# First norm of an image block: centring and variance moved between engines, and third-stage weights loaded in contiguous runs

## What is computed

```python
x = x + conv_ref(ln_c(x), ...)          # ln_c: norm over the 96 channels, eps 1e-6, no weights
t = to_tokens(x); x = from_tokens(t + ffn_ref(ln_t(t), W1, b1, W2, b2))
# conv_ref(v): crops of 16x16 pixels at a step of 14
#   y = layernorm(crop) * norm1_w + norm1_b            # eps 1e-5
#   4-head attention inside each crop, wproj, added back, overlaps averaged -> x2
#   y = gelu(layernorm(x2) @ fc1_w + fc1_b); dw = gelu(conv5x5(y) + dw_b)
#   result (y + dw) @ fc2_w + fc2_b + x2
# ffn_ref: values rounded to 8-bit (5 exponent bits) before each product, relu between W1 and W2
```

## Time and profile before

| | |
|---|---|
| runs | 9153.25, 9166.02, 9173.01 us; median 9166.02 |
| profiled execution | 9185.78 us, span 9184.0 us, mean granted TensorE clock 0.95 |
| busy share of the span | PE 87%, DVE 57%, ACT 51%, POOL 23% |
| first stage | 0 to 896 us |
| attention stage | 896 to 4599 us |
| third stage, head without strips | 4599 to 4709 us |
| third stage, strips | 4709 to 9184 us |

### The profile page before, as it was taken

One profiled execution on the slowest core, in us unless ns is written; L12 is line 12 of the kernel. 1 busy time (PEld: TensorE's weight loads), 2 busy tenths in 40 slices (PEclk: granted clock), 3 DMA queues, 4 the chain that ended last, 5 costly groups with the idle time before them and its releaser, 6 DMA issues.

```text
span 9184.0 us, 208496 instructions
## 1 busy us (share of the span) xinstructions
PE 8035.3 (87%) x76932; PEld 4839.5 (53%) x76932; DVE 5221.1 (57%) x9929; ACT 4672.3 (51%) x8702; POOL 2150.5 (23%) x1712
## 2 busy tenths in 40 slices
PE   6776899999999999999858989989989888998998
PEld 3333444444444444444445566666666666666665
DVE  5565677777777777777633444444444444444444
ACT  2221555555555555555525555555555555555554
POOL 0000333333333333333301211212111121121111
PEclk8888899999999999999969999999999999999999
DMA  4333343333433334333251111111111111111110
GB/s 119 113 114 104 88 98 87 91 94 84 100 83 94 94 84 98 86 92 94 71 45 34 44 40 34 44 40 35 43 40 43 35 43 41 34 44 40 35 43 24
DMA packets 480819, 612.84 MB, mean 67 GB/s; under 512 B 173263, under 2 KB 415697, under 8 KB 455317
## 3 DMA queue, kind: packets, MB, share of 16 engines
q1 hardware_dynamic: 480260, 605.46, 26.8%
HBM read 395.81 MB, written 166.64 MB: 61 GB/s over the span
## 4 chain that ended last, share of the span: by engine, by line
PE 28%; DVE 9%; ACT 7%; issue 5%; SPq 1%; DVEq 0%; ACTq 0%; DMA 0%; POOLq 0%; POOL 0%
PE P L1285 6%; PE P L1151 5%; PE P L1298 5%; PE P L1206 4%; ACT H L1358 4%; DVE H L1522 3%; PE P L1159 3%; DVE H L1515 2%; PE P L1314 2%; DVE Z L1537 2%; PE P L1125 1%; ACT Z L1383 1%; ACT L1383 1%; ACT L1346 1%; SPq L991 1%
## 5 line engine op out<-in xcount | busy, mean ns | idle before, releaser
L812 DVE TENSOR_REDUCE NM<-P 128x2 f32<-128x512 f32 x2888 | 1858.6, 686 | 719.2 <-PE P L645 714.3
L759 ACT ACTIVATE PROB<-P 128x512 f32<-128x512 f32 x2888 | 1491.1, 603 | 1090.7 <-PE P L660 1090.7
L1206 PE MATMUL P<-FC,XN 97*126 97x192 f32 x5408 | 1101.1, 343 | 15.7 <-ACT Y L1368 14.8
L1206 PEld LDWEIGHTS P<-FC,XN 97*126 97x126 f32 x5408 | 944.3, 197 | 167.9 <-issue 77.9
L660 PE MATMUL P<-QF,KS 32*128 32x256 f32 x11552 | 869.5, 417 | 94.0 <-DVE QF L806 93.2
L660 PEld LDWEIGHTS P<-QF,KS 32*128 32x128 f32 x11552 | 544.5, 192 | 642.0 <-DVE QF L806 506.6
L496 POOL TENSOR_TENSOR Y<-XHS,RNS 96x512 f32<-96x512 f32 x304 | 600.7, 2007 | 931.9 <-DMA RNS<-rnorm 931.9
L1352 ACT ACTIVATE SQ<-Z 96x512 f32<-96x512 f32 x260 | 163.8, 630 | 1286.5 <-DVE Z L1502 1286.5
L668 PE MATMUL P<-PROB,V 128*32 128x256 f32 x11552 | 797.8, 395 | 2.4 <-ACT PROB L759 1.5
L1368 ACT ACTIVATE Y<-P 126x384 f32<-126x384 f32 x1352 | 705.9, 570 | 109.2 <-PE P L1206 103.6
L1092 POOL TENSOR_TENSOR T<-T,Y 96x512 f16 (+1 forms) x260 | 299.2, 1151 | 1722.7 <-DVE Y L1526 1722.7
(11 more groups left out here) (141 smaller groups left out, 12209.9 us busy)
## 6 DMA issues: line engine op xcount, KB each, us to landing
RBC<-sums SPq DMA_DIRECT2D x456, 160.0 KB, 3.1
X<-x2map SPq DMA_DIRECT2D x52, 1344.0 KB, 8.4
XHS<-xhat SPq DMA_DIRECT2D x76, 768.0 KB, 6.4
RNS<-rnorm SPq DMA_DIRECT2D x38, 1536.0 KB, 9.2
x2map<-XHS SPq DMA_DIRECT2D x76, 768.0 KB
T<-in_x SPq DMA_DIRECT2D x52, 960.0 KB
out<-T SPq DMA_DIRECT2D x52, 960.0 KB, 4.9
X<-in_x SPq DMA_DIRECT2D x32, 1536.0 KB, 13.3
```

What stands on the lines that cost most here:

```text
L759: A.activation(PROB[:, par, u, :], P[:, B_ST[u], :], ACT.Exp, scale=DQ ** -0.5).then_inc(act_exp, 1)
L812: V_.tensor_reduce(NM[:, :, 32 * u + DQ], P[:, B_S[u], :].rearrange("p (a m) -> p a m", a=2), axis=AX.X, op=ALU.max).then_inc(dve_max, 1)
L1206: m = M.matmul(P[0:KW, 5 + (r + 2) % 3, i * MLP:(i + 1) * MLP], xnf[:, RI * WX * w:RI * WX * w + KW], FC1[:, :], start=True, stop=True)
```

## The change

**First stage.** TensorE multiplies the chunk by `CENW`, the identity minus 1/96 (made once by VectorE), and so has x minus mean in PSUM at once. ScalarE copies it out of PSUM to XH and squares it from PSUM to SQ; VectorE's `centre` is gone. The variance products go out four at a time, to 32 PSUM rows each (column groups), one bank; ScalarE copies the bank to SBUF (`VS`), and one product with `REP` sums the four groups and gives the three copies. Block i's spread products stand between the centring and variance products of block i+1 in TensorE's order. VectorE multiplies into buffers of their own (`XO`), and its second reciprocal comes behind the multiplications; ScalarE's second root of block i stands in the middle of block i+1. SP loads X for block i+3 once block i+1 has been centred (block i+2 before), and stores xhat before rnorm.

**Third stage.** W1, W2 and the filter are loaded as they lie (20 loads instead of 22), turned by eight fp32 transposes on TensorE into PSUM, and cast from there by VectorE; the tap products wait for those casts. The constants `stat` and `bcast` are gone; the first stage uses `pick`, `rep` and `spread` of the third.

```diff
+            def fetch(par, i):
+                b, j = where(i)
+                sp.dma_start(X[par][:, :], xv[:, b, bass.ds(j * TOK, TOK)].rearrange("c a n -> c (a n)")).then_inc(x_loaded[par], 16)
+
+            def keep(par, i):
+                b, j = where(i)
+                hold(sp, sp_passed, dve_xh, i * 8 + 8)
+                sp.dma_start(xhat[:, b, bass.ds(j * TOK, TOK)].rearrange("c a n -> c (a n)"), XO[par][:, :]).then_inc(stored[par], 16)
+                hold(sp, sp_passed, dve_rn, i + 1)
+                sp.dma_start(rv[:, b, bass.ds(j, 1), :].rearrange("c a i n -> c (a i n)"), RCP[0:NCH, 1, :]).then_inc(r_stored, 16)
+
+            sp.wait_ge(pe_cen, 8)
+            fetch(0, 2)
+            with sp.Fori(0, nblk // 2 - 2) as k:
                 for par in range(2):
                     i = k * 2 + par
+                    hold(sp, sp_passed, pe_cen, i * 8 + 16)
+                    fetch(1 - par, i + 3)
+                    keep(par, i)
...
+            def spread(i, j):
+                if j == 0:
+                    pe.wait_ge(dve_parts, i + 1)
+                if j >= 2:
+                    pe.wait_ge(dve_xh, i * 8 + (j - 1))
+                for c in (2 * j, 2 * j + 1):
+                    m = T.matmul(P[0:C, B_BC + j % 2, (c % 2) * CW:(c % 2 + 1) * CW], BSEL[:, c, :], RB[:, :], start=True, stop=True)
+                m.then_inc(pe_bc, 1)
+            def body(par, i, k):
+                pe.wait_ge(x_loaded[par], k * 16 + 16)
+
+                def centred(j):
+                    T.matmul(P[0:C, j % 4, :], CENW[:, :], X[par][:, pair(j)], start=True, stop=True).then_inc(pe_cen, 1)
+
+                def variance(q):
+                    pe.wait_ge(act_sq, i * 8 + (2 * q + 2))
+                    for g in range(4):
+                        c = 4 * q + g
+                        m = T.matmul(P[32 * g:32 * g + 32, B_VAR, 0:CW], SSEL[:, NV - 1 - c:NV - 1 - c + 32],
+                                     SQ[:, c // 2 % 4, (c % 2) * CW:(c % 2 + 1) * CW], start=(q == 0), stop=(q == 3))
+                    m.then_inc(pe_var, 1)
 
                 for j in range(4):
-                    mean(j)
-                for j in range(8):
-                    pe.wait_ge(act_sq, i * 8 + (j + 1))
-                    for c in (2 * j, 2 * j + 1):
-                        m = T.matmul(P[0:C, 4 + par, 0:CW], SSEL[:, c, :], SQ[:, j % 4, (c % 2) * CW:(c % 2 + 1) * CW],
-                                     start=(c == 0), stop=(c == NCH - 1))
-                    m.then_inc(pe_var, 1)
-                    if j < 4:
-                        pe.wait_ge(dve_cen, i * 8 + (j + 1))
-                        mean(j + 4)
-
...
+            def second_std(i):
+                act.wait_ge(dve_step, i * VSTEPS + 3)
+                if not first(i, 1):
+                    act.wait_ge(dve_rn, i)
+                A.activation(STD[:, 1, :], VR[:, :], ACT.Sqrt, bias=EPS[:, 1:2]).then_inc(act_std2, 1)
+
+            def body(par, i, k):
+                if not first(i, 2):
+                    act.wait_ge(dve_xh, i * 8 - 8)
                 for j in range(8):
-                    act.wait_ge(dve_cen, i * 8 + (j + 1))
+                    act.wait_ge(pe_cen, i * 8 + (j + 1))
+                    A.activation(XH[par][:, pair(j)], P[0:C, j % 4, :], ACT.Copy)
                     if j >= 4:
-                        act.wait_ge(pe_var, i * 8 + (j - 3))
-                    A.activation(SQ[:, j % 4, :], XH[par][:, pair(j)], ACT.Square).then_inc(act_sq, 1)
-                act.wait_ge(pe_var, i * 8 + 8)
-                A.activation(STD[:, :], P[0:C, 4 + par, 0:CW], ACT.Sqrt, bias=EPS[:, 0:1]).then_inc(act_std, 1)
-                act.wait_ge(dve_step, i * VSTEPS + 3)
-                A.activation(STD[:, :], VR[:, :], ACT.Sqrt, bias=EPS[:, 1:2]).then_inc(act_std, 1)
-
-            pipeline(act, front, lambda par, i: None)
+                        act.wait_ge(pe_var, i * 4 + (j // 2 - 1))
+                    A.activation(SQ[:, j % 4, :], P[0:C, j % 4, :], ACT.Square).then_inc(act_sq, 1)
+                    if j == 3 and not first(i, 1):
+                        second_std(i - 1)
+                act.wait_ge(pe_var, i * 4 + 4)
+                A.activation(VS[:, :], P[:, B_VAR, 0:CW], ACT.Copy).then_inc(act_vs, 1)
+                act.wait_ge(pe_rep, i + 1)
+                A.activation(STD[:, 0, :], P[0:C, B_STAT, 0:CW], ACT.Sqrt, bias=EPS[:, 0:1]).then_inc(act_std, 1)
+
+            blocks(act, body)
+            second_std(nblk - 1)
...
+            V.tensor_tensor(CENW[:, :], CENW[:, :], MEANW[:, :], ALU.subtract)
             V.tensor_copy(BSEL[:, :, :], BSEL32[:, :, :]).then_inc(dve_init, 1)
 
-            def centre(par, i):
-                for j in range(8):
-                    dve.wait_ge(pe_mean, i * 8 + (j + 1))
-                    V.tensor_tensor(XH[par][:, pair(j)], X[par][:, pair(j)], P[0:C, j % 4, :], ALU.subtract).then_inc(dve_cen, 1)
...
-                dve.wait_ge(act_std, i * 2 + 2)
-                if not isinstance(i, int) or i > 0:
-                    dve.wait_ge(r_stored, i * 16)
-                V.reciprocal(RCP[:, 1, :], STD[:, :]).then_inc(dve_rn, 1)
-
-            def back(par, i):
+                if not first(i, 2):
+                    dve.wait_ge(stored[par], k * 16)
                 for j in range(8):
                     dve.wait_ge(pe_bc, i * 8 + (j + 1))
-                    V.tensor_tensor(XH[par][:, pair(j)], XH[par][:, pair(j)], P[0:C, 6 + j % 2, :], ALU.mult).then_inc(dve_xh, 1)
-
-            centre(0, 0)
-            chain(0, 0)
-            with dve.Fori(0, nblk // 2 - 1) as k:
-                i = dve.snap(k * 2)
-                dve.wait_ge(stored[1], k * 16 + 16)
-                centre(1, i + 1)
-                back(0, i)
-                chain(1, i + 1)
-                dve.wait_ge(stored[0], k * 16 + 16)
-                centre(0, i + 2)
-                back(1, i + 1)
-                chain(0, i + 2)
-            dve.wait_ge(stored[1], (nblk // 2) * 16)
-            centre(1, nblk - 1)
-            back(0, nblk - 2)
-            chain(1, nblk - 1)
-            back(1, nblk - 1)
+                    V.tensor_tensor(XO[par][:, pair(j)], XH[par][:, pair(j)], P[0:C, B_BC + j % 2, :], ALU.mult).then_inc(dve_xh, 1)
+                dve.wait_ge(act_std2, i + 1)
+                if not first(i, 1):
+                    dve.wait_ge(r_stored, i * 16)
+                V.reciprocal(RCP[:, 1, :], STD[:, 1, :]).then_inc(dve_rn, 1)
+
+            blocks(dve, body)
...
-            with nc.allow_non_contiguous_dma(reason="weights, once"):
-                load(DW[0:25, :], dww.rearrange("c a y x -> (a y x) c"))
-                load(W1R, w1.rearrange("n k -> k n"))
-                for f in range(3):
-                    load(W2R[:, f, :], w2[:, f * 128:(f + 1) * 128].rearrange("n k -> k n"))
+            load(DWN, dww.rearrange("(h c) a y x -> c h (a y x)", h=2))
+            load(W1N, w1.rearrange("(f n) k -> n f k", f=3))
+            load(W2N, w2)
...
+            for f in range(3):
+                M.transpose(P[0:C, f, 0:128], W1N[:, f, :], IDN[:, :])
+                M.transpose(P[:, 3 + f, 0:C], W2N[:, f * 128:(f + 1) * 128], IDN[0:C, 0:C])
+            for h in range(2):
+                t = M.transpose(P[0:25, 6, h * C:(h + 1) * C], DWN[:, h, :], IDN[0:C, 0:C])
+            t.then_inc(pe_turn, 1)
+            pe.wait_ge(dve_step, 1)
...
-            V.tensor_copy(W1Q[:, :], W1R, saturate=False)
-            V.tensor_copy(W2Q[:, :, :], W2R, saturate=False)
+            dve.wait_ge(pe_turn, 1)
+            V.tensor_copy(W1Q[:, :].rearrange("k (f n) -> k f n", f=3), P[0:C, 0:3, 0:128], saturate=False)
+            V.tensor_copy(W2Q[:, :, :], P[:, 3:6, 0:C], saturate=False)
+            V.tensor_copy(DW[0:25, :], P[0:25, 6, 0:MLP])
```

More of the change, by code:

```diff
@@ L44, in norm_stage @@
         XH = [sb(f"XH{i}", [C, TOK]) for i in range(2)]
+        XO = [sb(f"XO{i}", [C, TOK]) for i in range(2)]
         SQ = sb("SQ", [C, 4, 2 * CW])
-        STD = sb("STD", [C, CW])
+        VS = sb("VSA", [128, CW])
+        STD = sb("STD", [C, 2, CW])
         VR = sb("VR", [C, CW])
@@ L110, in _ @@
+                    fetch(1 - par, i + 3)
+                    keep(par, i)
+            for i in range(nblk - 4, nblk):
+                if i + 3 < nblk:
+                    sp.wait_ge(pe_cen, i * 8 + 16)
+                    fetch((i + 3) % 2, i + 3)
+                keep(i % 2, i)
             sp.wait_ge(r_stored, 16 * nblk)
             for par in range(2):
-                sp.wait_ge(stored[par], 16 * (nblk // 2 + par))
-        def pipeline(eng, front, back):
-            front(0, 0, None)
+                sp.wait_ge(stored[par], 16 * (nblk // 2))
@@ L117, in pipeline, with blocks @@
+        def blocks(eng, body):
+            body(0, 0, 0)
+            body(1, 1, 0)
             with eng.Fori(0, nblk // 2 - 1) as k:
                 i = eng.snap(k * 2)
-                front(1, i + 1, k)
-                back(0, i)
```

(46 more changed lines are left out.)

68 lines of the change are left out of this document (28 added, 40 removed).

## The result

The changed kernel takes **9362.34 us** (median of 4 runs, 9278.71 to 9380.12) beside 9159.64 us for the kernel before on the same chip: ratio 1.0195, 95% interval 1.0152 to 1.0238. It is slower by about 2% (1.5 to 2.4), where 8704 us and a clear gain were forecast. Its profiled execution took 9361.24 us, span 9359.4, mean granted clock 0.902 (0.95 before).

The account below looks back on a forecast made before the run. The first stage was taken as bound by a dependence loop through three engines, the third stage's head by weight loads. Savings of 416 and 46 us, 462 together, gave 8704 us from the median 9166.02; 80% range 8665 to 8800.

Parts of the forecast that it names:

- First stage: Term for the first stage: it ends at 479.6 us in place of 895.9, 416 us less.
- a walk of 13.91: First stage, step-by-step estimate of one block's dependence loop through the engines: 13.91 us a block.
- DMA pace: Rival, first stage: loads and stores set the pace, 15 us a block, +34 us, 8738; blocks stretched to 16 had 0.19.
- column groups in a row: Rival, first stage: variance column groups don't overlap, 1.72 us a group, 16.9 a block, +93 us, 8797; chance 0.06.
- clock in this stage: Rival, first stage: TensorE stays at 1.2 GHz for all (+220, 8924) or a third (+70, 8775) of each block; chance 0.09.
- table loads: Rival, first stage: ScalarE's Copy and Square evict each other, 16 loads a block, 127 us slower than before, 9293.
- Head of the third stage: Term for the third stage's start: weights land 49.5 us sooner, 3 us lost again, 46 us less; bounds 40 and 52.
- Attention 3703 as before: Attention stage: its code is kept, so it stays 3703 us long.
- The step that failed: Attention and the rest of the third stage, strips included: they keep their code, so no time was added for them.
- The two foreseen terms: First stage 416 us less and third stage's weights 46 us less, together 462 us.
- table loads or another loss: Case for the whole kernel: slower than before through ScalarE's table loads in the first stage or another loss; chance 0.02.

Follow-up runs that it names:

- run 10: The kernel before with 214 empty VectorE instructions ahead of its attention loop: 9123.40 us, ratio 0.9932, attention 3659.6 us.
- run 11: run 1's kernel with 128 empty VectorE instructions ahead of its attention loop: 8678.23 us, ratio 0.9429, attention 3687.3 us.
- run 2: The kernel before with 28 empty TensorE instructions ahead of the third stage's weight wait: 9857.04 us, ratio 1.0733.
- run 1: The changed kernel with 128 empty TensorE instructions (half a block) ahead of the third stage's weight wait: 8670.12 us, ratio 0.9436 to the kernel before.
- runs 5, 6: Empty TensorE instructions ahead of the third stage: 256 in the changed kernel, 9364.46 us, ratio 1.0205; 22 in the kernel before, 9814.81 us, ratio 1.0664.
- run 7: run 1's kernel with 28 empty TensorE instructions at the head of the strip loop's body: 9387.75 us, ratio 1.0200.
- run 4: The kernel before with only the new third-stage weight loads and transposes, first stage old: 9123.28 us, ratio 0.9931.

## Why the prediction was wrong, point by point

- **First stage: right.** A steady block, the timeline of the changed kernel:

```profile
209.59 1.69 DVE L229 RECIPROCAL RCP<-STD 96x256 f32<-96x256 f32 x1
...
215.05 0.64 PE L158 MATMUL P<-SQ,SSEL 96*32 96x256 f32 x8
215.62 1.96 PE L152 MATMUL P<-X,CENW 96*96 96x512 f32 x4
...
217.83 2.48 DVE L245 TENSOR_TENSOR XO<-XH,P 96x512 f32<-96x512 f32 x4 [1.61 <-PE P L145]
```

  The next chain starts at 223.41: 13.82 us, which is also the mean of the stage's 31 periods, against a walk of 13.91. VectorE's long gap is 1.61 us and stands before its third multiplication. A variance group is 0.57 us to the next product (0.62 taken from the earlier trace rows). ScalarE's copy takes 613 ns and its square 618 (0.59 taken). The stage ends at 477.5, forecast 479.6.
- **DMA pace, column groups in a row, clock in this stage, table loads:** none came. X lands 8.9 us after its issue (13.3 in the earlier trace rows), the stage's clock is 0.98 over its length, and it has two table loads.
- **Head of the third stage: right.** VectorE's first cast and first tap copy:

```profile
4152.43 1.56 DVE L1461 CAST BSEL<-Z 96x2688 bf16<-96x2688 f32 x1 [17.64 <-DMA Y<-in_L_ffn_b]
...
4157.24 3.08 DVE L1474 COPY WC<-P 127x192 f32<-127x192 f32 x5 [0.51 <-PE P L1132]
```

  W1 and W2 are issued in 1.31 us (49.28 in the earlier trace rows). From the end of attention to the cast are 18.2 us (65.3 before), 47.1 less where 49.5 were taken; the copy comes 4.8 us after the cast (6 taken). In all 44.3 us less, forecast 46.
- **Attention 3703 as before: wrong by 46.5 us**, to the good. Moving VectorE's code does it (run 10), by something that acts along the whole stage. The mechanism is open; run 11 was meant to say and didn't.
- **The step that failed** is the one that had no working: "The attention stage between them and the rest of the third stage keep their code", and so the sum adds 416 and 46 and nothing for the strips. They took 684.6 us more, against 462 foreseen as the whole gain. They keep their code but not its place. Shown: the place alone brings the loss (run 2) and takes it away (run 1), by blocks (runs 5, 6); the gap alone brings the low clock (run 7). Not shown is the memory's size and rule of replacement; seven blocks against eight fits in the main, but it isn't the whole rule, since 4 to 11 of 50 jumps stay free with eight and one in 50 is not with seven (kernel before and run 4). What goes with the gap each time is the late packet.
- With that term gone the sum holds for the parts that it has. Run 1's span of 8664.5 is 519.5 below 9184.0: first stage 417.7, head 44.3, attention 39.1, and 18.4 in the strips, of which 11.5 are the second strip's gap and low clock (96.7 against 85.2 us), also gone. The two foreseen terms give 462.0, the forecast figure. That it agrees so closely is luck: the first stage gave 1.7 us more than forecast and the head 1.7 less.
- None of the rivals was this one. The case slower than before (table loads or another loss) had 2%. The trace of before held the sign: instruction packets as a queue of their own on the page, and a strip of 96.7 us among strips of 85.2.

## What to carry to other kernels

A change also moves the code behind it. Where a loop's body is near the size that an engine's instruction memory holds, look in the profile for the instruction queue's packets during the loop and for idle time "<-issue" at the jump back, and count how many 16,384 B blocks the loop touches before and after; if that number grows and the signs are there, pad ahead of the loop, in a place where the engine waits anyway (here 128 instructions beside a wait for weights, worth 7.4%). Measure each part alone before a good part is given up for a loss that isn't its own. And price a gap of TensorE by what follows it: here 3 us of idleness at the head of a strip cost 14.

## What the hardware showed that wasn't expected

- A TensorE loop of 1646 instructions is fetched again at none or one of its 50 ways back with 0, 12 or 16 instructions added ahead of it (strips of 85.1 to 85.4 us), and at 39 to 41 of them with 22 or 28 (97.0 and 97.3). Each time goes with nine packets of 16,384 B: one 4.3 to 9.4 us before the jump's first product, eight from the gap on.
- 2.75 to 3.3 us without work on TensorE, once in 85 us, is followed by 24 to 34 us at 1.2 GHz, fetch or no fetch.
- VectorE's code, moved by 214 instructions, made an unchanged stage of 3703 us 44 us shorter, with the same 319 instruction packets.
- Four fp32 products in column groups of 32 with 256 columns pass in 0.57 us to the next full-array product, where two passes of 256 columns are 0.43 at full clock: switching to column groups and back costs 0.14 us at most.
